# Building the selection of a group's 18th edge tile ahead of VectorE's other work on the group

## The reference

```
h = layernorm(x)
for two layers:
    agg = segment_sum(h[src], dst)            # one row per edge is fetched and summed by destination
    h   = relu(h @ W_self + (agg / max(deg, 1)) @ W_neigh + b)
x = x + h
logits = layernorm(x) @ Wg                    # two of eight experts are taken for each node
x = x + sum over the two experts of gate * layernorm_e(relu(x @ W1_e + b1_e) @ W2_e + b2_e)
```

## Time and profile before

| | us |
|---|---|
| median of 3 runs | 3316.79 |
| the runs | 3334.26, 3314.17, 3316.79 |
| the profiled execution | 3312.28 |
| its span, first to last instruction | 3310.5 |
| mean granted clock of PE over the span | 0.900 of full speed |

### The profile page before, as it was taken

The page is one execution under the profiler, slowest core; times in us unless marked ns, Lnnn a source line. Parts: engine busy times, 40 slices in busy tenths (PEclk is TensorE's granted clock), DMA queues, the critical chain, the costliest instruction groups (busy, mean ns, idle before and its releaser), DMA issues. The chain is left out here.

```text
span 3310.5 us, 57698 instructions
## 1 busy us (share of the span) xinstructions
PE 2537.0 (77%) x12092; PEld 1591.9 (48%) x12093; DVE 1381.3 (42%) x3740; ACT 837.6 (25%) x1611; POOL 2013.5 (61%) x2229
## 2 busy tenths in 40 slices
PE   0177777777777777578778888877778799999997
PEld 0044334334343344244444444444444577778875
DVE  8522222222222222134333443334343667666765
ACT  6311111111111111011111111111111355555554
POOL 0366666666666665466666666666664366666665
PEclk9988888988989888789888988889899899999998
DMA  7568788888877666577766777667775576656643
GB/s 277 194 196 257 241 271 254 263 257 254 269 247 228 184 186 182 191 214 214 221 201 212 223 212 217 211 200 221 213 218 178 142 166 142 128 110 138 140 80 64
DMA packets 239296, 663.39 MB, mean 200 GB/s; under 512 B 47224, under 2 KB 48818, under 8 KB 236168
## 3 DMA queue, kind: packets, MB, share of 16 engines
q0 software_dynamic: 151472, 464.79, 50.9%
q10 hardware_dynamic: 62388, 128.09, 11.2%
q1 hardware_dynamic: 25380, 69.89, 6.5%
HBM read 550.93 MB, written 111.69 MB: 200 GB/s over the span
## 5 line engine op out<-in xcount | busy, mean ns | idle before, releaser
L720 POOL DMA_INDIRECT store_all<-xn_scratch,srcT x782 | 777.9, 995 | 534.0 <-issue 210.5
L720 POOL DMA_INDIRECT store_all<-h_scratch,srcT x782 | 768.4, 983 | 458.3 <-SPq L613 213.4
L1328 DVE TENSOR_TENSOR sel<-iota_g,dstT 128x384 f16<-128x384 f32 (+1 forms) x602 | 317.1, 530 | 1442.4 <-PE ps L1777 843.9
L1776 PE MATMUL ps<-store_all,sel 128*128 x1680 | 701.7, 418 | 82.2 <-issue 38.3
L1777 PE MATMUL ps<-store_all,sel 128*128 x1680 | 702.5, 418 | 12.6 <-issue 12.3
L1747 PE MATMUL ps<-wts,sT 128*128 128x512 f32 x1176 | 474.1, 518 | 187.8 <-DVE sT L1351 145.9
L1747 PE MATMUL ps<-wts,aT 128*128 128x512 f32 x1176 | 430.3, 477 | 156.9 <-DVE aT L1357 140.5
L1747 PEld LDWEIGHTS ps<-wts,sT 128*128 128x128 f32 x1176 | 254.1, 224 | 299.7 <-DVE sT L1351 168.1
L1747 PEld LDWEIGHTS ps<-wts,aT 128*128 128x128 f32 x1176 | 227.7, 207 | 256.7 <-DVE aT L1357 169.2
L1776 PEld LDWEIGHTS ps<-store_all,sel 128*128 128x128 f16 x1680 | 179.6, 107 | 296.1 <-issue 229.0
L1747 PE MATMUL ps<-wts,m_hT 128*128 (+1 forms) x1224 | 313.3, 405 | 4.8 <-DVE m_hT L1623 4.2
(11 more groups left out here) (296 smaller groups left out, 3080.5 us busy)
## 6 DMA issues: line engine op xcount, KB each, us to landing
expert_weights_scratch<-w_both ACTq DMA_DIRECT2D x64, 512.0 KB
wts<-expert_weights_scratch SPq DMA_DIRECT2D x64, 512.0 KB
store_all<-in_L_ffn_W ACTq DMA_DIRECT2D x64, 256.0 KB
self_t<-xn_scratch ACTq DMA_DIRECT2D x49, 256.0 KB
self_t<-h_scratch ACTq DMA_DIRECT2D x49, 256.0 KB
store_all<-in_x ACTq DMA_DIRECT2D x49, 256.0 KB
store_all<-xn_scratch,srcT POOLq DMA_INDIRECT x782
store_all<-h_scratch,srcT POOLq DMA_INDIRECT x782
```

The costliest lines, as they stand in the source:

```text
L720: pool.indirect_dma_start(rows[:, t % SLOTS, :], None, rows_d, bass.IndirectOffsetOnAxis(ap=srcT[:, t:t + 1], axis=0)).then_inc(s_rows[t % ...
L1328: dve.tensor_tensor(sel[:, k:k + w, :], iota_g[:, p, :].unsqueeze(1).to_broadcast([P, w, P]), dstT[:, bass.ds(t, w)].unsqueeze(2).to_broad ...
L1776: pe.matmul(agg_p[p], sel[:, k, :], row[:, 0:D], start=k == 0, stop=False)
```

## The change

In DVE's `tile` of group g the number of extra tiles of group g is now read first. If there is one, the selection of the 18th tile is built at once, ahead of the hooks and of the selections of group g + 1. Behind the group's work only a 19th tile and more are still built, in a loop that is entered under a condition of its own, and the wait for the last of them (`loop_end`) stays there. PE's code keeps its order; its branch is only renamed.

```diff
             def tile(g, p, more={}):
                 steps = step and not (isinstance(g, int) and g + ahead >= NT)
+                if ahead:
+                    e0, n = tiles_of(g)
+                    with eng.If_lt(eng.to_reg(0), eng.to_reg(n)):
+                        step(ST, g, p, value(eng, cell(tab_extra, g), NT * ET), within(e0 + ST, ETP - 1))
                 if steps:
-                    t0, n = tiles_of(g + ahead)
+                    t0, m = tiles_of(g + ahead)
                 if opening:
                     opening(g, p)
...
-                if step:
-                    if ahead:
-                        t0, n = tiles_of(g)
+                if ahead:
                     with eng.If_lt(eng.to_reg(0), eng.to_reg(n)):
                         x0 = value(eng, cell(tab_extra, g), NT * ET)
-                        with eng.Fori(0, n) as j:
+                        with eng.If_lt(eng.to_reg(1), eng.to_reg(n)):
+                            with eng.Fori(1, n) as j:
+                                step(ST, g, p, x0 + j, within(e0 + ST + j, ETP - 1))
+                        loop_end(x0 + n)
+                elif step:
+                    with eng.If_lt(eng.to_reg(0), eng.to_reg(m)):
+                        x0 = value(eng, cell(tab_extra, g), NT * ET)
+                        with eng.Fori(0, m) as j:
                             step(ST, g, p, x0 + j, within(t0 + ST + j, ETP - 1))
-                        if loop_end:
-                            loop_end(x0 + n)
                 if tail:
                     tail(g, p)
```

## The result

The changed kernel takes 3294.39 us (median of 20 runs) against 3324.64 us for the kernel before (20 runs beside them). The ratio is 0.9912 with a 95% interval of 0.9893 to 0.9931, so the change is worth 29 us, 23 to 36. The forecast was 3309 us and within 1% of before.

A forecast was written before the change was run, and what follows sets the result against it. No engine is always busy; handoffs set the layers' pace, so only waits PE cannot make up for count. Gains 13 + 18 less costs 14, 5 and 5 give 7 us: 3316.8 - 7, about 3309 us, range 3276 to 3337.

The forecast's parts named there:

- rival 2: PE's waits before the fourteen 18th tiles are lost time in full: 80.8 us, about 3236 us; chance 0.05.
- The one more condition: Added condition in each of DVE's 98 groups, 0.3 us each; cost 4 us in first layer, 1 us in second.
- The second layer's gain: Removing PE's wait for the 18th selection there gains 13 us, between 9.4 and 16.4.
- the pairs: Seven 18-tile groups per layer, each with its follower: 356.41 and 352.34 us, 21.5 and 16.4 us over undisturbed groups.
- The first layer's costs: Work around DVE's divisor delays PE's aggregate transposes: 14, 5 and 4 us against a gain of 18 us.
- The two terms for the head: First layer, ahead of DVE's divisor: 5 us for read, condition and selection in 18-tile groups, 4 us for every group's condition.
- The follower's term: First layer, group after an 18-tile group: later divisor makes PE wait for the aggregate, 2 us each, 14 us in all.
- Rival 1: The pairs fall to the undisturbed pace at a clock of 0.93: 38 us gain, about 3279 us; chance 0.13.
- the clock rule: Long idle stretches between matmul bursts reset PE's clock to half rate; by it alone 37.5 us of busy time returns.
- the undisturbed pace: Length of a group not disturbed by an 18th tile: 23.92 us in the first layer, 23.99 in the second.
- Rival 3: Slower: added condition and reads at DVE's head delay the divisor or `moments`; 35 us, about 3352; chance 0.10 with harder form.
- the harder form: DVE's added branch must fetch instructions in 98 groups: 55 us, about 3372 us; chance 0.10 together with Rival 3.

The follow-up runs named there:

- e8: The kernel before with the edges of the 18th tiles left out of the sums, reads and conditions kept; ratio 0.9895, 35 us faster.
- e5: The kernel before with four more table reads ahead of the 18th selection in the fourteen groups that have one; ratio 1.0137, 46 us slower.
- e6: The kernel before with the change's table reads and condition at DVE's head of a group, the 18th selection still behind; ratio 0.9982, 6 us faster.
- e1: The change in the second layer alone, the first as in the kernel before; ratio 0.9919 to the kernel before, 27 us faster.
- e2: The change in the first layer alone, the second as in the kernel before; ratio 0.9971 to the kernel before, 10 us faster.
- e4: The changed kernel unaltered, measured again; ratio 0.9892 to the kernel before.
- e10: The changed kernel unaltered, measured a third time on another chip; ratio 0.9925 to the kernel before.
- e7: The changed kernel with three more table reads at DVE's head of every group; ratio 1.0019 to the kernel before, some 36 us more than the change.
- e11: The kernel before with only its second read of tab_tile moved from the end of DVE's group to position 10; ratio 0.9932, 23 us faster.

## Why the prediction was right, and where its sizes were not

**Right.** The forecast held its class and its range. Its gain of 7 us was a quarter of the measured 29, so the class owes much to its width, 33 us to either side. *The wait goes at all fourteen places*: 80.8 to 4.2 us. *sT is late next, and the tile falls into that wait*: the dense product follows sT by 0.06 to 0.71 us in the first layer's seven groups; in the second four follow by 0.06 us, and three by 1.07 to 2.08, over the 1 us that was named. *The lateness is worth far less than 80.8 us, because the long wait takes the place of the ordinary ones*: e8, which has no such tile at all, gains 35 us, and rival 2 (3236 us) is out. e5 is the complement, which the prediction did not have: past that cover each us counts. *The one more condition is nearly free*: e6, as a net figure.

**The second layer's gain was mis-sized**: 13 us with 16.4 as the upper bound, measured 27 (17 to 37) in e1. In the profile after it is 20.3. The bound counted the excess of the pairs in one execution. They do fall as forecast, by 9.5 us to 342.82 (339 was named); but the 31 other groups fall too, from 751.65 to 742.40, about as much. That the other groups gain from the change is not shown by this, because e2, whose second layer is that of the kernel before, has as little there. Its windows, sum of the pairs of the second layer, then of the other groups:

```profile
sum 363.49, PE 280.81; mean PE 40.12
...
sum 742.14, PE 589.52; mean PE 19.02
```

By the prediction's own reckoning the excess of these pairs is 363.49 - 335.9 = 27.6 us instead of 16.4, and e1 gained 27. On the chip of e1, e2 and e4 the pairs fall from 363.49 to 350.42 and 348.91, the others from 742.14 to 738.94 and 736.79. So the term was read too small from one execution, in which less of the layer's time lay in the pairs than in e2. How the time splits between pairs and others differs from run to run (332.53 and 756.77 in e8); their sum is steadier: 1104.0 and 1105.6 us with the waits (before, e2), 1085.2, 1089.4 and 1085.7 without them (after, e1, e4).

**The first layer's costs were mis-sized**: 18 of gain less 14 + 5 + 4 made a loss of 5 us; e2 measured a gain of 10 (2 to 17). The two terms for the head, 5 and 4 us, come to 1 us at most by e6, net and without the selection itself. The follower's term of 14 us was too large: its wait before the transposes was to grow from 1.4 to 3 to 5 us, and it is 2.6 us in the profile after (17.9 us over seven followers, 8.8 of them at one), 2.1 in e2, 0.7 in e4 and 0.4 in e10. The mechanism is there (2.86 us in the timeline of group 23 above), but not in every run, and e2 says that it cost less than its length, or the gain beside it was larger; the two were not told apart. The idle time before the divisor was to rise by 0.3 us. In the profile after it does, from 1.32 to 1.58 us in the median of the 49 groups; in e2, e4 and e10 it is 1.31, 1.32 and 1.21, so that agreement was luck.

**Rival 1's time, not its mechanism.** 29 us is nearer to the 38 of rival 1 than to the 7 of the forecast. But rival 1 had the busy time of PE come back with the clock, and that did not happen. In the pairs PE's busy time falls by 9.1 + 5.5 = 14.6 us, and in the other groups it rises by 21.6 + 3.5 us; over both layers it is 1804.83 us (1789.58 in e4, 1816.30 in e10) against 1797.67. The granted clock of the layers goes from 0.87 to 0.86 and from 0.88 to 0.89. By the prediction's estimate, the clock rule that it weighed, from the Trainium skill (TensorE: Matmul & The Clock Gate, "Why this matters for your kernels"), would have brought 37.5 us of busy time back; the measurement has none of it in the sum of the layers. The pairs of e4 in the first layer do come down to 336.66 us, almost the 334.9 of the undisturbed pace, with PE as busy in them as before (37.09 us a pair against 37.43). Nor did the pace of 23.9 us, on which the pairs were measured, hold in every execution: the other groups of the first layer take 693.31 / 28 = 24.8 us instead of 24.1, and 24.6 in e4, but 24.0 in e2, which has the same first layer. The prediction named undisturbed groups that leave 23.9 us as a sign against itself, and in two of these three executions the first layer shows it.

**Rival 3.** Its soft form did not occur in the change, but e7 shows that it is real: 1.4 us more at the head of a group, and the change's whole gain is gone. The change adds 78.5 - 71.1 = 7.4 us of idle time there in 49 groups, 0.15 each, in the profile after, and none in e4 and e10 (70.6 and 64.7 us), which is what kept the rival away. Of the harder form the page of the kernel after shows this:

```profile
q14 instruction: 40, 0.32, 0.0%
```

That is 3 packets more than in the earlier trace rows, in all 98 groups together: the added branches did not make DVE's loops fetch their instructions again. The Trainium skill's stall of a taken branch (Runtime: NRT & Kernel Launch, "Instruction fetch mechanics") was not met here.

**What stays open.** The first layer of the same code varies between 1152.8 and 1171.4 us in one execution each, and no row tells what decides it. The stretch of the experts, which the change does not touch, took 740.1 us in the profile before and 746.5 after. Why the granted clock of the layers stayed, although the long waits went, was not tried.

## What to carry to other kernels

A wait before one instruction is worth what it adds to the stretch up to where the engines are in step again, not its own length: here 29 to 36 us of 80.8, but all of what was added on top. To size it, leave the waiting work out in one run and lengthen the wait in another. When an engine's work is moved, look for the place with slack in the middle of its round, since its end is the head of the next round, where table reads of the sequencer were paid for here (e7, e11). Windows of a single execution do not size such a gain: the same code's pairs lay 11 us apart in two.

## What the runs showed of the hardware that was not expected

One read of a table by DVE's sequencer takes longer than the selection it serves: four more reads in e5 added 57.3 - 20.4 = 36.9 us of idle time over fourteen places, 36.9 / 56 = 0.66 us each, and three more in e7 added 69.5 us over 49 groups, 69.5 / 147 = 0.47 us each, against 0.29 us for the selection. And an instruction that waits for PE's work can start some us after the end that the profile models for that work. In the kernel before, ACT's high half of the nodes' own rows waits for their transposes:

```profile
871.50 0.61 PE L1792 MATMUL ps<-down,self_t 128*128 128x128 bf16 x8
...
873.74 0.88 ACTq L920 DMA_DIRECT2D expert_weights_scratch<-w_both  x2
...
877.01 0.60 ACT L938 ACTIVATE sT<-ps 128x512 fp32r<-128x512 f32 x1 [10.45 <-remote]
```

The transposes end at 872.11 by the profile and ACT starts at 877.01, after 10.45 us idle. Up to 874.62 ACT's sequencer still issues two transfers; for the 2.4 us from there on the view shows no work that it could have waited for. No run was made to find the cause. It is one reason to trust the sums of windows more than single waits.
